# Evacuations ahead of the low part, in a two-layer graph convolution in split fp32

## What is computed

```
d   = (sum(adj, axis=1) + 1e-9) ** -0.5
msg = (d[:, None] * adj * d[None, :]) @ x          # for x and for spatial_x
H   = relu(msg @ W + b)                            # H_f and H_s
a   = sigmoid(concat(H_f, H_s) @ W_att + b_att)
out = layernorm(x + a * H_f + (1 - a) * H_s)
```

## Time and profile before

| | |
|---|---|
| median of 3 runs | 423.37 us (422.57 to 423.82) |
| the profiled execution, its time / its span | 422.08 us / 420.0 us |
| TensorE busy | 374.0 us (89%) |
| VectorE busy | 291.8 us (69%) |
| ScalarE busy | 285.4 us (68%) |
| GpSimd busy | 171.1 us (41%) |
| low parts (L417), 70 instructions | 152.3 us |
| evacuations (L440), 112 instructions | 71.3 us, 680 ns each |
| DMA, mean over the span | 132.84 MB, 316 GB/s |

### The profile page before, as it was taken

The page is one execution under the profiler, slowest core; times in us unless marked ns, Lnnn a source line. Parts: engine busy times, 40 slices in busy tenths (PEclk is TensorE's granted clock), DMA queues, the critical chain, the costliest instruction groups (busy, mean ns, idle before and its releaser), DMA issues.

```text
span 420.0 us, 5140 instructions
## 1 busy us (share of the span) xinstructions
PE 374.0 (89%) x1680; PEld 308.0 (73%) x1680; DVE 291.8 (69%) x377; ACT 285.4 (68%) x338; POOL 171.1 (41%) x222
## 2 busy tenths in 40 slices
PE   0779998699969999999899989999999999988950
PEld 0567887488758887888688868888888888867740
DVE  2579983596466966597646966488656669398895
ACT  3768588887888749887888597674533672657545
POOL 1103001021000881068101999150001947889975
PEclk9999999999989999999999999999999999998985
DMA  8999999999999999999999999897655353240002
GB/s 311 388 424 424 417 421 420 422 421 420 421 423 421 414 343 423 424 422 419 421 421 421 411 417 385 313 374 275 226 185 183 137 179 123 101 151 27 25 26 75
DMA packets 25529, 132.84 MB, mean 316 GB/s; under 512 B 2848, under 2 KB 7712, under 8 KB 11296
## 3 DMA queue, kind: packets, MB, share of 16 engines
q1 hardware_dynamic: 25504, 132.53, 78.9%
HBM read 130.42 MB, written 2.10 MB: 316 GB/s over the span
## 4 chain that ended last, share of the span: by engine, by line
DMA 31%; PE 30%; POOL 16%; ACT 8%; DVE 7%; issue 5%; SPq 1%; POOLq 0%; DVEq 0%; ACTq 0%
DMA nat<-in_adj 18%; DMA raw<-in_At 13%; PE sums L352 10%; PE sums L353 10%; PE sums L354 10%; POOL S L678 6%; ACT Ah L537 4%; ACT nat L550 4%; POOL fin L689 3%; DVE Al L417 3%; POOL fin L684 2%; POOL xs L685 2%; POOL vare L694 2%; DVE xs L467 1%; POOL rstd L697 1%
## 5 line engine op out<-in xcount | busy, mean ns | idle before, releaser
L352 PE MATMUL sums<-Ah,Yh 128*128 128x512 f32 x512 | 202.5, 395 | 26.8 <-DVE Yl L428 18.1
L417 DVE TENSOR_TENSOR Al<-raw,Ah 128x2048 fp32r<-128x2048 f32 (+1 forms) x70 | 152.3, 2180 | 99.8 <-ACT Ah L537 99.6
L354 PE MATMUL sums<-Al,Yh 128*128 128x512 f32 x512 | 200.8, 392 | 0.0
L353 PE MATMUL sums<-Ah,Yl 128*128 128x512 f32 x512 | 200.7, 392 | 0.0
L537 ACT ACTIVATE Ah<-raw 128x2048 fp32r<-128x2048 f32 (+1 forms) x70 | 123.4, 1768 | 59.8 <-PE sums L354 28.6
L352 PEld LDWEIGHTS sums<-Ah,Yh 128*128 128x128 f32 x512 | 97.1, 190 | 50.5 <-DVE Yl L428 19.3
L550 ACT ACTIVATE nat<-nat 128x2048 f32<-128x2048 f32 x53 | 101.6, 1916 | 18.8 <-DMA nat<-in_adj 17.5
L354 PEld LDWEIGHTS sums<-Al,Yh 128*128 128x128 f32 x512 | 96.9, 189 | 20.5
L353 PEld LDWEIGHTS sums<-Ah,Yl 128*128 128x128 f32 x512 | 97.0, 190 | 19.7
L440 DVE TENSOR_TENSOR acc<-sums,acc 128x512 f32<-128x512 f32 x112 | 71.3, 680 | 6.7 <-PE sums L354 6.7
L643 POOL TENSOR_SCALAR dg<-rs 128x1 f32<-128x1 f32 x22 | 14.2, 644 | 150.3 <-ACT nat L550 150.0
(11 more groups left out here) (40 smaller groups left out, 130.9 us busy)
## 6 DMA issues: line engine op xcount, KB each, us to landing
raw<-in_At SPq DMA_DIRECT2D x63, 1024.0 KB, 10.1
nat<-in_adj SPq DMA_DIRECT2D x56, 1024.0 KB, 11.5
xs<-in_xs SPq DMA_DIRECT2D x7, 512.0 KB, 11.2
out<-xs SPq DMA_DIRECT2D x32, 64.0 KB, 1.6
raw<-in_At SPq DMA_DIRECT2D x4, 256.0 KB, 10.3
xs<-in_xs SPq DMA_DIRECT2D x1, 384.0 KB, 9.2
xs<-in_xs SPq DMA_DIRECT2D x1, 128.0 KB, 2.4
watt<-in_W_att SPq DMA_DIRECT2D x1, 128.0 KB, 10.2
```

The source lines that it names most:

```text
L352: pe.matmul(to, Yh[:, t % YRING, hs], high, start=first, stop=False)
L353: pe.matmul(to, Yl[:, t % YRING, hs], high, start=False, stop=False)
L354: mm = pe.matmul(to, Yh[:, t % YRING, hs], low, start=False, stop=last)
L417: dve.tensor_tensor(Al[:, k % SPLITS, a * IB:b * IB], raw[:, k % RAWS, a * IB:b * IB], Ah[:, k % SPLITS, a * IB:b * IB], ALU.subtract).the ...
```

## The change

VectorE's loop decides otherwise which evacuations go ahead of low(k). Before, up to item 15 all that are due went first, and from item 16 on only the first of four that ended together; all others went behind low(k). After, all go first in every item up to 47. At the start, the first two runs (they end in item 1) are evacuated ahead of low(2) instead of low(3). From item 48 on nothing is changed, and nothing on the other engines.

```diff
             for k in range(K):
                 ended = [e for e in evac_order if end_item[e] == k - 2]
-                while ended and k < 2 * G:
+                if k == 3:
+                    ended = ended[2:]
+                while ended and k < FINAL:
                     evacuate(ended.pop(0))
-                if len(ended) == GT:
-                    evacuate(ended.pop(0))
+                if k == 2:
+                    for e in evac_order[:2]:
+                        evacuate(e)
                 if k == 1:
                     own_share(3)
                 low(k)
```

## The result

The changed kernel takes 426.54 us (median of 7 runs, 424.68 to 427.07); the kernel before, on the same chips, 422.80 (7 runs, 422.07 to 423.82). The ratio is 1.0074, with a 95% interval of 1.0059 to 1.0089: slower by 3.7 us. The profiled execution of the changed kernel is one of its quicker ones, 425.17 us (span 423.1 us); against the profiled one of before, that is 3.1 us.

A forecast was written before the change was run, and what follows sets the result against it. The data stream was taken to bound the kernel up to item 40, TensorE behind it. Gains of 7.7 us were absorbed; +2.1 (collisions) and +1.6 (clock) gave +3.7 on the median 423.37: 427.1 us, range 422.8 to 428.6.

The forecast's parts named there:

- What goes: TensorE's idles inside items 16 and 32, the slow clock at 120 to 125 us, 1.2 us at item 2: 7.7 us.
- Nothing of it reaches the end: Up to item 40 the data's pace does not change, so the 7.7 us gained earlier are all absorbed.
- Point 1: At item 37 all eight evacuations go first, 4.9 us, so low(37) runs 2.2 us late, 230.4 to 232.7.
- Points 2 to 4: Items 38 and 39: low parts collide with GpSimd's block sums or degree, making row 23's D 2.1 us late.
- points 2 and 3: Item 38: low(37) stretches GpSimd's first sum (+1.8), low(38) blocks the third; the fourth ends at 240.2 (+2.0).
- No change: Rival, 21%: sums and low parts interleave otherwise, D stays near 241.3 and item 40 at 250.5; 423.4 us.
- Point 5: ScalarE waits for D, so high(40) and TensorE's item 40 come 2.1 us later, as do loads of items 43, 44.
- Point 6: TensorE's idle ahead of item 40 grows to 3.4 us, and the clock falls behind it: +1.6 us.
- More lost: Rival, 7%: collision in items 21 to 24 delays item 26's load, the queue runs dry: another 1.5 us, 428.6.
- the prediction's 1.2: GpSimd's block sum blocked by a low part ends 1.2 us behind that part, as measured at item 38.
- its other value: A blocked GpSimd sum runs its whole 1.3 us after the low part, making the shift 2.3 instead of 2.1.

The follow-up runs named there:

- e2: Changed kernel, but at items 21, 29 and 37 only the first of four runs is evacuated ahead of the low part: 422.67 us, ratio 0.9993.
- e5: Changed kernel without GpSimd's four block sums of item 38: 423.28 us, ratio to the kernel before 1.0012.
- e7: Changed kernel with ScalarE's row sums of parts 48 and 49 ahead of its y_high of row 23: 425.56 us, ratio to before 1.0063.
- e8: Changed kernel with 12 short filler matmuls in TensorE's idle ahead of item 40: 426.21 us, ratio to before 1.0077.
- b1: Changed kernel's evacuation order, with parts 48 to 55 loaded and summed up to two items later and GpSimd's two groups one item later: 424.72 us.
- b2: Same later parts and groups as b1, but evacuations ahead of low only at items 16, 17, 24, 25, 32, 33, and two runs ahead of low(2): 424.21 us.
- e3: Kernel before, with evacuations ahead of low also at items 16, 17, 32 and 33 alone: 422.90 us, ratio 0.9999.
- e1: Kernel before, with all four runs evacuated ahead of low(37) at item 37 alone: 425.80 us, ratio 1.0067.
- e4: Kernel before, without GpSimd's four block sums of item 38: 422.44 us, ratio 0.9988.
- b0: Kernel before, evacuations unchanged, with parts 48 to 55 loaded and summed up to two items later and GpSimd's two groups one item later: 424.30 us.
- e9: Kernel before, with all four runs evacuated ahead of low(21) at item 21 alone: 424.13 us, ratio 1.0035.

## Why the prediction was right

The median came out at 426.54 for 427.1, and 3.7 us above the median of before, as forecast, but the parts of the sum were not all right. Step by step:

- *What goes* was right: the idles of 16 and 32 and the slow clock behind the first are gone. Item 2 gained 0.4 us in the profiled execution, where I had 1.2 (0.9 to 1.5 in e2, e5, e7, e8, b1 and b2). *Nothing of it reaches the end*: right, and e2 and e3 show it.
- Point 1 was right: eight evacuations in 4.87 us, low(37) 2.1 us later behind low(36) than before (7.4 for 5.3 us).
- Points 2 to 4, the collisions, were worth +2.1 and measured +1.7 in the profiled execution (9.24 for 7.48 us, and the degree as before). The first and the third sum were stretched, as points 2 and 3 said. e1, e2, e4 and e5 show that this group of four and these sums cost the time. How many of GpSimd's instructions are hit is a near tie, as the rival "No change" said: in e1 three sums were hit and the degree was not, and GpSimd added 1.1 us, not 1.7.
- Point 5 was right for the way by D. That the loads of items 43 and 44 are a way of their own fits e7, but its gain is within the noise.
- Point 6, the clock behind item 40 (+1.6), failed for the profiled execution: 2.93 us of idle, and the clock stayed full. In e1 it fell behind 2.90 us, and 1.7 us of that execution's loss are the clock. It can happen there, but e8 speaks against its making the median of the changed kernel. The mean granted clock points the same way: 0.963 to 0.973 in the five runs from 426.08 us up, 0.971 and 0.972 in the two quick ones.
- In its place stands what I had only as the rival "More lost", at 7%: a collision ahead of the loads of items 25 and 26 makes the stream run thin between 147 and 162 us. It is on the degree and not on the sums, and it is not made up, which I had expected by item 32. I wrote that the queue is never empty, and that DMA is 1.01 busy at 420 GB/s in every stretch; both failed, and the second was wrong for the kernel before already (0.93 and 368 GB/s in 147 to 162 us). Item 38's data came 1.1 us later in the profiled execution. In the traces of three other kernels with the changed order (e8, e5, e7), high(36) starts at 222.35 to 223.39 us instead of 220.86, so the lag there is 1.5 to 2.5 us. With 1.7 for the sums that is 3.2 to 4.2, which would cover the median's 3.7. That is an argument from few traces; the executions near the median left none themselves.

So the place, the sign and the first mechanism were right. The total was right by luck: a term that mostly isn't there (the clock, 1.6) had about the size of one that I had left out (the stream, 1.1 to 2.5).

## What to carry to other kernels

Before an engine's work is put in another order, list what runs beside each moved instruction, and who waits for that: here an operation with two SBUF inputs moved by 2 us fell on another engine's sums, and the price was paid by a load and by a third engine. An idle of the busiest engine is worth its length only if nothing downstream waits for data; the first place where it does (here item 40) decides. A load stream that is full on average can still be starved by a late issue or two, and moving other loads out of a tight stretch (b0) need not be a relief.

## What the hardware showed that I had not expected

- GpSimd's sum under a low part does not run its whole time behind it: in the changed kernel both stretched sums end some 1.15 us behind the low part, as before, against 1.3 us for a whole sum alone, which decides for the prediction's 1.2 and against its other value. A collision costs up to 2.0 us (the longest sum took 3.28), and three of the four sums of an item can be hit (7.48, 9.24 and 10.60 us for four, with one, two and three).
- The clock does not follow the length of an idle alone. It stayed full behind 2.93 us in the changed kernel and fell to half behind 2.90 (e1, 0.72 in the stretch) and behind 2.84 us (ahead of item 25, 0.66). In other traces it stayed full behind 2.82 us (e7, ahead of item 25, 1.00 in 166 to 171) and fell behind 1.87 (b0) and 0.87 us (e7, ahead of item 43). So two idles near 3.4 us in one trace were too few to tell from.
- A gap in a stream that is full from then on is not made up. 0.6 MB were missing by 162 us in the changed kernel, and from 170 to 250 us both kernels moved 419 GB/s. Which loads are late for it differs: in the changed kernel high(31) and high(32) start when they did before and high(33) 1.1 us later; in e9, with a gap of 0.8 MB, high(28), high(31), high(32) and high(33) are all 1.5 to 1.7 late. Why they differ stays open.
